# Attention weights in four layers: the clip of the scores replaced by a min with the adjacency

## The reference

```
e   = s1[:, None] + s2[None, :]              # s1 = h @ a1 (rows), s2 = h @ a2 (neighbours), h = relu(layernorm(x)) @ W
e   = where(e > 0, e, 0.2 * e)               # leaky relu
att = softmax(where(adj > 0, e, -9e15), axis=-1)
x   = x + f(att @ h)                         # f: elu (layers 0, 2, 3) or gelu (layer 1); layer 0 then @ W_out + b_out
```

## Time and profile before

| what | us |
|---|---|
| median of three runs | 768.17 (767.72 to 768.95) |
| the profiled execution: its time | 767.65 |
| its span, first to last instruction | 766.0 |
| TensorE busy | 745.2 |
| VectorE busy | 628.0 |
| ScalarE busy | 327.6 |
| mean granted TensorE clock | 0.995 |

### The profile page before, as it was taken

One profiled execution on the slowest core, in us unless ns is written; L12 is line 12 of the kernel. 1 busy time (PEld: TensorE's weight loads), 2 busy tenths in 40 slices (PEclk: granted clock), 3 DMA queues, 4 the chain that ended last, 5 costly groups with the idle time before them and its releaser, 6 DMA issues.

```text
span 766.0 us, 15942 instructions
## 1 busy us (share of the span) xinstructions
PE 745.2 (97%) x6443; PEld 727.3 (95%) x6443; DVE 628.0 (82%) x1050; ACT 327.6 (43%) x886; POOL 16.1 (2%) x36
## 2 busy tenths in 40 slices
PE   8899999999999999999999999999889989998997
PEld 8789999999999999999999999999779979996997
DVE  4997879797787968879787797878688959997986
ACT  5876551452543336134354324633440254435420
POOL 3000000000000000000000000000000000000000
PEclk9999999999999999999999999999999999999999
DMA  9794000000000000000000000000000000000001
GB/s 298 263 357 186 29 28 2 27 0 27 27 1 27 0 27 3 24 27 0 27 12 15 27 0 27 0 0 1 2 1 2 1 1 1 2 1 1 1 22 36
DMA packets 13874, 29.39 MB, mean 38 GB/s; under 512 B 1296, under 2 KB 7568, under 8 KB 13840
## 3 DMA queue, kind: packets, MB, share of 16 engines
q1 hardware_dynamic: 11152, 20.00, 7.6%
q0 software_dynamic: 2688, 8.92, 3.3%
HBM read 27.80 MB, written 1.11 MB: 38 GB/s over the span
## 4 chain that ended last, share of the span: by engine, by line
PE 85%; ACT 5%; DVE 5%; DMA 3%; issue 1%; POOL 0%; DVEq 0%; ACTq 0%; POOLq 0%
PE acc L408 49%; PE acc L431 25%; PE side L508 3%; PE side L364 3%; DMA stage<-in_adj_t_dram 3%; ACT adjT L623 2%; PE acc L378 1%; PE acc L482 1%; DVE probs L1082 1%; ACT hpT L716 1%; PE side L470 1%; DVE stats L1284 0%; PE side L456 0%; DVE xn L1328 0%; ACT fill L701 0%
## 5 line engine op out<-in xcount | busy, mean ns | idle before, releaser
L408 PE MATMUL acc<-V,probs 128*128 128x129 f32 x3840 | 438.3, 276 | 1.9 <-DVE probs L1076 1.9
L408 PEld LDWEIGHTS acc<-V,probs 128*128 128x128 f32 x3840 | 434.2, 192 | 4.9 <-ACT V L657 2.7
L1082 DVE SCALAR_TENSOR_TENSOR probs<-rho,t_now,adjT 128x1024 f32<-128x1024 f32 x224 | 272.9, 1277 | 11.3 <-PE acc L408 9.1
L1178 DVE SCALAR_TENSOR_TENSOR probs<-rho,t_now,adjT 128x768 f32<-128x768 f32 (+3 forms) x179 | 146.7, 879 | 9.6 <-PE acc L431 6.6
L716 ACT ACTIVATE hpT<-rows 32x256 f32<-32x256 f32 x224 | 92.8, 414 | 69.5 <-DVE rows L1119 67.0
L431 PEld LDWEIGHTS acc<-stage,probs 128*128 128x128 f32 x1024 | 115.0, 192 | 4.0 <-ACT stage L874 3.7
L431 PE MATMUL acc<-stage,probs 128*128 128x129 f32 x1024 | 116.1, 275 | 2.1 <-DVE probs L1178 2.1
L431 PE MATMUL acc<-V,probs 128*128 128x129 f32 x768 | 89.4, 275 | 1.0 <-DVE probs L1178 1.0
L431 PEld LDWEIGHTS acc<-V,probs 128*128 128x128 f32 x768 | 87.4, 192 | 2.0 <-ACT V L874 1.8
L701 ACT ACTIVATE fill<-mean_now,empty 128x128 f32<-128x128 f32 x120 | 36.7, 394 | 87.9 <-DVE den L1095 87.8
L1127 DVE TENSOR_TENSOR X<-X,side 128x512 f32<-128x512 f32 x28 | 19.3, 688 | 63.5 <-PE side L508 63.5
(11 more groups left out here) (190 smaller groups left out, 409.4 us busy)
## 6 DMA issues: line engine op xcount, KB each, us to landing
stage<-in_adj_t_dram SPq DMA_DIRECT2D x32, 512.0 KB, 6.7
rho<-rho_dram POOLq DMA_DIRECT2D x15, 512.0 KB, 3.7
X<-in_x_dram SPq DMA_DIRECT2D x2, 512.0 KB, 4.5
W0t<-in_W_t_dram SPq DMA_DIRECT2D x1, 512.0 KB, 5.2
W<-in_L_gnn_W_heads_dram SPq DMA_DIRECT2D x1, 512.0 KB, 6.4
Wout<-in_L_gnn_W_out_dram POOLq DMA_DIRECT2D x1, 512.0 KB, 9.3
out_dram<-X SPq DMA_DIRECT2D x1, 512.0 KB, 4.5
out_dram<-X SPq DMA_DIRECT2D x1, 384.0 KB, 3.9
```

The lines of the kernel that those rows point to most:

```text
L408: last = nc.tensor.matmul(group(c, k), probs[:, j % RING, k * P:(k + 1) * P], V[:, j, :], start=(j == 0 and k % PER_BANK == 0), stop=(j == ...
L1082: nc.vector.scalar_tensor_tensor(probs[:, j % RING, :], rho[:, c * CH:(c + 1) * CH], t_now[:, j:j + 1], adjT[:, j, c * CH:(c + 1) * CH], A ...
L1178: return nc.vector.scalar_tensor_tensor(slot_of(n, p, j)[:, first:end], rho[:, at + first:at + end], t_now[:, j:j + 1], adjT[:, j, at + fi ...
```

## The change

A rho that isn't clipped only exceeds 1 where s1 + c is negative, and there the maximum has to be 1. As adj is 0 or 1 and t is at most 1, the weight can be written as min(max(rho, t), adj). So in all lines that make weights `ALU.mult` becomes `ALU.min`, and:

- rho, t and v come from the scores directly: ScalarE's exponential takes the scores and a bias column -0.8 c or -0.2 c. The VectorE lines 1034 for head 0, 1059, 1065, 1353 and 1364 go (`r_of_first_head`, `r_rows_of_heads`, `exponent_rows`, `late_d`). The maximum is spread with `ident_neg`, -0.8 on the diagonal, and reduced with min to `neg_c`, whose second column is a quarter of it.
- at the start head 0's maximum is spread alone by one matmul, into its own bank. The transposition for the eight heads follows; its second matmul (`spread_max_of_heads`) and `center_of_heads` move behind tiles 1 and 3 of the first unit, and ScalarE's `factors` behind the eighth cast. The cast of block 3 moves behind the first scaling of V.
- v is written straight into V's last column (no copy), and V's first tile is scaled by VectorE.
- the second half of rho comes right behind t and v on ScalarE; the second tile's weights are made in two halves too.
- on TensorE `rows_of_heads(0)` moves from tile 5 to tile 7 and `mean_rows` of the first unit from tile 9 to tile 14.

```diff
+            nc.gpsimd.affine_select(out=ident_neg[:, :], in_=ident_neg[:, :], compare_op=ALU.not_equal, fill=-(1 - ALPHA),
...
             def first_spread_max():
 
                 pe.wait_ge(cmax_ready, 1)
+                pe.wait_ge(ident_neg_ready, 1)
+                pe.wait_ge(first_copied, NB)
+                nc.tensor.matmul(first_max_bank, cmax[:, 0:1].to_broadcast([P, P]), ident_neg[:, :],
+                                 start=True, stop=True).then_inc(first_maxT_psum, 1)
                 nc.tensor.transpose(first_scores[0:H, FT:FT + P], cmax[:, :], ident[:, :]).then_inc(cmaxT_psum, 1)
+
+            def spread_max_of_heads():
+
                 pe.wait_ge(c_row_ready, 1)
...
-            unit(0, 0, 0, ((1, lambda: rows_of_heads(1)), (5, lambda: rows_of_heads(0)),
-                           (9, lambda: mean_rows(1, W0[:, :, :].rearrange("p h d -> p (h d)"), H, r_ready, 6)),
+            unit(0, 0, 0, ((1, spread_max_of_heads), (1, lambda: rows_of_heads(1)), (7, lambda: rows_of_heads(0)),
+                           (14, lambda: mean_rows(1, W0[:, :, :].rearrange("p h d -> p (h d)"), H, rho_ready, 6)),
...
+            def first_factors():
+
+                act.wait_ge(neg_c_ready, 2)
+                nc.scalar.activation(V[:, :, D], s2_all[:, :, 0], ACT.Exp, bias=neg_c_rep[:, 1:2], scale=ALPHA).then_inc(first_vexp, 1)
+                nc.scalar.activation(t_now[:, :], s2_all[:, :, 0], ACT.Exp, bias=neg_c_rep[:, 0:1], scale=1 - ALPHA).then_inc(first_t_ready, 1)
...
             def rho_exp(count, c, heads, which=(0, 1)):
-                r_buf = rho_rows if heads > 1 else rho
+                r_buf, bias = (rho_rows, neg_c_row) if heads > 1 else (rho, neg_c_rep)
+                act.wait_ge(neg_c_ready, 3 if heads > 1 else 1)
                 for k in (2 * c + i for i in which):
-                    act.wait_ge(r_ready, count + k % 2 + 1)
-                    nc.scalar.activation(r_buf[:, k * 512:(k + 1) * 512], r_buf[:, k * 512:(k + 1) * 512], ACT.Exp,
-                                         scale=-(1 - ALPHA)).then_inc(rho_ready, 1)
+                    act.wait_ge(s1_psum, count + k % 2 + 1)
+                    nc.scalar.activation(r_buf[:, k * 512:(k + 1) * 512], side[0:H if heads > 1 else P, k % 2, :], ACT.Exp,
+                                         bias=bias[:, 0:1], scale=-(1 - ALPHA)).then_inc(rho_ready, 1)
...
-            cast(2, 4)
-            factors()
+            cast(2, 3)
             rho_exp(0, 0, 1, (0,))
-            act.wait_ge(tv_ready, 2)
-            nc.scalar.activation(V[:, :, D], v_all[:, 0, :], ACT.Copy)
+            first_factors()
+            rho_exp(0, 0, 1, (1,))
             act.wait_ge(first_copied, NB)
+            act.wait_ge(first_vexp, 1)
             first_scale_v(0)
-            cast(4, 6)
+            cast(3, 6)
             first_scale_v(1)
             cast(6, 8)
+            factors()
...
             def late_factors(n):
 
-                act.wait_ge(late_d_ready, n)
-                nc.scalar.activation(t_now[:, :], late_d[:, :], ACT.Exp, scale=1 - ALPHA).then_inc(late_t_ready, 1)
-                nc.scalar.activation(v_now[:, :], late_d[:, :], ACT.Exp, scale=ALPHA).then_inc(late_vexp_ready, 1)
+                act.wait_ge(late_c_ready, 2 * n - 1)
+                nc.scalar.activation(t_now[:, :], scores[:, :], ACT.Exp, bias=neg_c[:, 0:1], scale=1 - ALPHA).then_inc(late_t_ready, 1)
+                act.wait_ge(late_c_ready, 2 * n)
+                nc.scalar.activation(V_of[n % 2][:, :, D], scores[:, :], ACT.Exp, bias=neg_c[:, 1:2], scale=ALPHA).then_inc(late_vexp_ready, 1)
                 late_rho(n, 0)
+                late_rho(n, 1)
                 act.wait_ge(late_vexp_ready, n)
-                nc.scalar.activation(V_of[n % 2][:, :, D], v_now[:, :], ACT.Copy)
-                scale_late_v(n, 0, 1)
-                late_rho(n, 1)
                 scale_late_v(n, 1, 4)
...
+                dve.wait_ge(first_maxT_psum, 1)
+                nc.vector.tensor_reduce(neg_c_rep[:, 0:1], first_max_bank, AX.X, ALU.min).then_inc(neg_c_ready, 1)
+                dve.wait_ge(neg_c_ready, 1)
+                nc.vector.tensor_scalar(neg_c_rep[:, 1:2], neg_c_rep[:, 0:1], ALPHA / (1 - ALPHA), None, ALU.mult).then_inc(neg_c_ready, 1)
...
+                dve.wait_ge(first_copied, 1)
+                dve.wait_ge(first_vexp, 1)
+                nc.vector.tensor_scalar(V[:, 0, 0:D], V[:, 0, 0:D], V[:, 0, D:D + 1], None, ALU.mult).then_inc(first_v, 1)
...
-            unit(0, 0, rho_and_adj(0, 0, True), ((5, lambda: r_rows_of_heads(1)), (6, lambda: mean(0, 1)), (9, lambda: r_rows_of_heads(0)), (12, add_bias),
-                                                   (15, first_t)), t_all[:, 0, :])
+            unit(0, 0, rho_and_adj(0, 0, True), ((3, center_of_heads), (6, lambda: mean(0, 1)), (12, add_bias)))
...
             def late_center(n):
 
                 dve.wait_ge(late_maxT_psum, n)
-                link(nc.vector.tensor_reduce(late_c[:, :], max_bank, AX.X, ALU.max))
-                nc.vector.tensor_scalar(late_d[:, :], scores[:, :], late_c[:, 0:1], None, ALU.subtract).then_inc(late_d_ready, 1)
-
-            def exponent_rows(n, k):
...
+                nc.vector.tensor_reduce(neg_c[:, 0:1], max_bank, AX.X, ALU.min).then_inc(late_c_ready, 1)
+                dve.wait_ge(late_c_ready, 2 * n - 1)
+                nc.vector.tensor_scalar(neg_c[:, 1:2], neg_c[:, 0:1], ALPHA / (1 - ALPHA), None, ALU.mult).then_inc(late_c_ready, 1)
+                dve.wait_ge(late_vexp_ready, n)
+                v0 = V_of[n % 2][:, 0, :]
+                nc.vector.tensor_scalar(v0[:, 0:D], v0[:, 0:D], v0[:, D:D + 1], None, ALU.mult).then_inc(late_v0_ready, 1)
```

More of the change, by code:

```diff
@@ L396, in unit @@
                         pe.wait_ge(rows_ready, 2 * u - 1)
-                    first = j == 0 and isinstance(u, int) and u == 0
-                    if first:
+                    first = j < 2 and isinstance(u, int) and u == 0
+                    if first and j == 0:
                         pe.wait_ge(first_v, 1)
-                        pe.wait_ge(first_half, 1)
                     elif c == 0 and (j % 4 == 0 or isinstance(u, int) and u == 0 and j == 1):
                         pe.wait_ge(v_ready, q * 4 + j // 4 + 1)
-                    if not first:
+                    if first:
+                        pe.wait_ge(first_half, j + 1)
+                    else:
                         pe.wait_ge(probs_ready, u * NT + j + 1)
@@ L653, in first_scale_v @@
             def first_scale_v(g):
-                for t in range(4 * g, 4 * g + 4):
+                for t in range(max(4 * g, 1), 4 * g + 4):
                     where = V[:, t, 0:D] if t < NK + 1 else first_group(t)[:, 0:D]
[L657 to L660, removed]
+                    last = nc.scalar.activation(V[:, t, 0:D], where, ACT.Copy, scale=V[:, t, D:D + 1])
                 last.then_inc(v_ready, 1)
+            def first_factors():
+                act.wait_ge(neg_c_ready, 2)
+                nc.scalar.activation(V[:, :, D], s2_all[:, :, 0], ACT.Exp, bias=neg_c_rep[:, 1:2], scale=ALPHA).then_inc(first_vexp, 1)
+                nc.scalar.activation(t_now[:, :], s2_all[:, :, 0], ACT.Exp, bias=neg_c_rep[:, 0:1], scale=1 - ALPHA).then_inc(first_t_ready, 1)
             def factors():
@@ L865, in late_rho @@
                 to = rho[:, k * 512:(k + 1) * 512]
-                act.wait_ge(late_r_ready, 4 * (n - 1) + k + 1)
-                nc.scalar.activation(to, to, ACT.Exp, scale=-(1 - ALPHA)).then_inc(late_rho_ready, 1)
+                if k < 2:
+                    act.wait_ge(s1_kept, 2 * n - 1 + k)
+                    s1_rows = to
+                else:
+                    act.wait_ge(late_s1_psum, 4 * (n - 1) + k + 1)
+                    s1_rows = side[:, k % 2, :]
+                nc.scalar.activation(to, s1_rows, ACT.Exp, bias=neg_c[:, 0:1], scale=-(1 - ALPHA)).then_inc(late_rho_ready, 1)
             def scale_late_v(n, first, end):
@@ L1073, in unit @@
                         dve.wait_ge(summed, u * NT + j - RING + 1)
-                    if j == 0 and isinstance(u, int) and u == 0:
-                        dve.wait_ge(rho_ready, 1)
-                        nc.vector.scalar_tensor_tensor(probs[:, 0, 0:512], rho[:, 0:512], t_now[:, 0:1], adjT[:, 0, 0:512],
-                                                       ALU.max, ALU.mult).then_inc(first_half, 1)
-                        dve.wait_ge(rho_ready, 2)
-                        nc.vector.scalar_tensor_tensor(probs[:, 0, 512:CH], rho[:, 512:CH], t_now[:, 0:1], adjT[:, 0, 512:CH],
-                                                       ALU.max, ALU.mult).then_inc(probs_ready, 1)
+                    if j < 2 and isinstance(u, int) and u == 0:
+                        if j == 0:
+                            dve.wait_ge(first_t_ready, 1)
+                        for k, done in enumerate((first_half, probs_ready)):
+                            dve.wait_ge(rho_ready, k + 1)
```

(8 more changed lines are left out.)

91 lines of the change are left out of this document (42 added, 49 removed).

## The result

The changed kernel takes 769.44 us (median of 20 runs, 767.57 to 772.61), the kernel before 767.63 in the 20 runs beside them: ratio 1.0025, interval 1.0017 to 1.0033. I had forecast 766.8 and held anything above 768.4 unlikely. Beside the later experiments both were timed again: 1.0019 (1.0009 to 1.0030). One execution of the start's part with the mean's row after tile 9 (experiment 3) fell into a slow state, 1288 us at a granted clock of 0.557, and its ratio leaves it out.

What follows compares the result with a forecast made beforehand. TensorE, busy 745 of 766 us, bounds the kernel; only its roughly 20 us of standing can give. Late layers 0.9 plus hpT 0.5 make 1.4 us off 768.17, so 766.8; range 765.3 to 768.4.

Steps and rivals of the forecast that it cites:

- The late layers: Three late layers' beginnings: first tile 0.16 us earlier, second tile's 0.14 us stall gone; 0.30 a layer, 0.9 in all.
- The bias's price: ScalarE's exponentials: a bias column adds 0.08 to 0.09 us each; the 512-wide one takes 709 ns against 626.
- The start up to the first tile: First unit: rho on ScalarE at 20.36 instead of 21.77, TensorE's first weighted matmul near 22.45, 1.0 us earlier.
- rival A: Clock stays up at the start, bias costs nothing: late layers 1.4 us, ScalarE's chain 1.0 to 1.6 earlier; 765.4; chance 0.22.
- The wait for the mean's row: ScalarE in the first unit waits 2.7 to 4.4 us for the row moved behind later tiles, holding back casts and loads.
- its effect on hpT: Before the first output projection: hpT comes 0.3 to 0.7 us earlier, 0.5 taken, and TensorE carries that lead.
- my case without a fall: Start with the clock not fallen: mean's row done at 55.1, ScalarE ready by 52.4, waiting 2.7 us.
- The load of block 27: Start's load for the 28th block: issued at 59.2, must land within 3.8 us; estimated 3.3 us, in time.
- The step that failed: Start: TensorE's 1.0 us lead at the first tile can't be kept, as it already stands for hpT at 81.88.
- Rival C: Start: waiting for the mean starves the loads, the 28th block lands 3.7 us later; 2.8 us slower, 771.0; chance 0.10.

Runs made afterwards that it cites:

- experiment 3: Changed lines put into the kernel before by part: start's 770.31 us, late layers' 766.55 us, start's with the mean's row after tile 9 766.39 us.
- late only: Only the late layers' part of the change put into the kernel before: 766.55 us, 0.9987.
- version 6: Changed kernel with the mean's row after tile 9 and useless matmuls in two standstills of each late layer: 764.06 us, 0.9944; again 763.97 us, 0.9952.
- experiment 2: Kernel before with only the first unit's mean's row moved from after tile 9 to after tile 14: 772.23 us, 1.0047.
- the start alone: Only the start's part of the change put into the kernel before: 770.31 us, 1.0034.
- experiment 1: Changed kernel with the first unit's mean's row after tile 9 instead of tile 14: 765.05 us, 0.9963 of the kernel before.

## Why the prediction was wrong

Where the time of the profiled executions goes, cut at four kinds of instruction (us; a star: the clock fell in it):

| stretch | before | change | mean's row at 9 | late only | before, row at 14 | version 6 |
|---|---|---|---|---|---|---|
| to the first projection | 81.88* | 81.61 | 78.61 | 81.55* | 86.17* | 80.23* |
| to the first late spread | 476.86* | 478.26* | 476.81* | 476.71 | 478.26* | 477.51* |
| spread to second tile, layer 1 | 5.26 | 5.25* | 4.94 | 5.52* | 5.56* | 4.94 |
| the same, layer 2 | 5.25 | 5.52* | 6.42* | 4.94 | 5.56* | 4.94 |
| the same, layer 3 | 5.25 | 4.94 | 4.94 | 4.94 | 5.25 | 4.94 |
| first late spread to the end | 207.2 | 207.0 | 208.0 | 206.6 | 207.9 | 206.1 |
| span | 766.0 | 766.8 | 763.5 | 764.9 | 772.3 | 763.8 |

The falls in the first row lie near 24 us (before, row at 14) or 12 us (late only, version 6). Those in the second lie near 550 us, ahead of the late layers, and cost little, but for the two of 478.26, which have theirs behind the first projection.

**The late layers: right where the clock stays up, which in the change it does in one layer of three.** Predicted 0.30 us a layer, as 0.16 at the first tile and 0.14 at the second. Where the clock stays up it is 5.25 to 4.94 = 0.31, as 0.17 and 0.14. The terms are in the rows of the third late layer: reduce at 702.44, t_now at 702.76 (0.31 us, 0.21 without a bias), rho at 703.18, half tile at 704.03, TensorE at 704.92, which is 3.08 us after the spread instead of 3.25. The bias's price is that of the rows:

```profile
L901 ACT ACTIVATE rho<-rho,neg_c 128x512 f32<-128x512 f32 x6 | 4.0, 708 | 0.0
```

708 ns against 626, an Exp now, so the Trainium skill's rule ("ScalarE: Activation LUTs", section "What ACT_TABLE_LOAD costs"), some 93 ns for each pointer operand, holds for it within 11 ns. As a whole the late part gave 1.0 us in experiment 3, against 0.9 predicted. What I left out of it is the clock: in the beginnings of layers 1 and 2 it fell in all three profiles of the change, and there the exponent scores (four matmuls, 1.9 us) take 3.0 to 3.5 and end last instead of the half tile. So from the first late spread to the end the three profiles of the change gain 0.2 to 0.3 us on the one of before, not 0.9.

```profile
630.51 0.49 PE L520 MATMUL acc<-ident_neg,late_max 128*128 128x128 f32 x2 [0.40 <-DVE late_max L1376]
630.83 3.52 PE L512 MATMUL side<-hT,waL 128*128 128x512 f32 x4
634.14 2.28 PE L453 MATMUL acc<-V,probs 128*128 128x129 f32 x18
```

In the kernel before, its one profile has no fall there, but the profiles of experiment 2 and of the start alone, both with the late layers of before, have two each, so I can't say that the change makes them more frequent.

**The start up to the first tile: right.** Predicted: rho at 20.36, half tile near 21.55, TensorE near 22.45, ninth cast at 31.4. Measured 20.36, 21.57, 22.47, 31.31:

```profile
20.36 0.69 ACT L700 ACTIVATE rho<-side,neg_c_rep 128x512 f32<-128x512 f32 x1 [0.83 <-DVE neg_c_rep L1064]
...
21.57 2.74 DVE L1115 SCALAR_TENSOR_TENSOR probs<-rho,t_now,adjT 128x512 f32<-128x512 f32 x4
...
22.47 3.81 PE L428 MATMUL acc<-V,probs 128*128 128x129 f32 x32 [1.50 <-DVE probs L1115]
```

The clock didn't fall behind the shorter standstill, so TensorE won another 1.3 us. My forecast had worked out both cases; rival A (0.22) counted on this one.

**The wait for the mean's row: right in place, and its effect on hpT near.** Predicted 2.7 to 4.4 us of wait, measured 4.66: the row was done as in my case without a fall (55.59, I had 55.1), but ScalarE stood ready at 50.9 and not 52.4, so the wait is 2 us longer than the 2.7 I had for that case. Block 22's cast came at 57.05 (58.3 predicted), block 27's at 61.97 (63.0), hpT 0.3 us earlier (0.3 to 0.7; in the other two profiles of the change 0.4 earlier and not at all). The load of block 27 took 3.8 us, an estimated 3.3 in the prediction; the fixed cost in that estimate is one that the Trainium skill ("DMA: Bandwidth & Descriptors", section "Anatomy of one DMA") gives for DMAs issued by GpSimd, while SyncE issues these. Then the last two casts wait for their loads, 0.8 us in all, where I had them back to back:

```profile
67.74 1.06 ACT L647 ACTIVATE adjT<-stage 128x1024 bf16<-128x1024 int32 x1 [0.48 <-DMA stage<-in_adj_t_dram]
69.15 1.06 ACT L647 ACTIVATE adjT<-stage 128x1024 bf16<-128x1024 int32 x1 [0.35 <-DMA stage<-in_adj_t_dram]
```

**The step that failed** is the sentence "TensorE near 22.45: 1.0 us earlier. But TensorE then has a lead it can't keep: at 81.88 it stands already for hpT". It priced the lost lead at nothing. A lead that can't be kept is a longer standstill, 1 us to 3, and behind it the clock falls in a stretch that has no slack: 1.4 us in the profile. With it the account of the profile closes: 1.4 us faster were predicted, 0.8 slower came; of these 2.2 us the fall takes 1.4, the late layers' missing gain 0.6 and hpT's 0.2. And the lead could be kept: with the row after tile 9 (experiment 1) nothing of it is lost, so the standstill was the price of the moved row. I had the fall at 24 us in front of me and asked only whether it would come again at the start, where it costs nothing; I didn't ask where the next standstill goes. Rival C named the right place, the wait for the mean starving the loads, but let it pay through a late block 27, and I gave it a chance of 0.10. In the change that load came in time and the next ones cost 0.8 us. Experiment 2 shows how near the edge the forecast stood: there ScalarE comes to the wait at 53.9 and not 50.9, the row comes 2.4 us later too (TensorE starts its tiles 1.1 us later and its clock falls at 24 us), and rival C's mechanism makes 2.9 us of waits for loads.

**What stays open.** By profile the change is 0.8 us slower, by median 1.8 (20 runs) and 1.4 (12 runs). So some 0.6 to 1 us of the loss is in no profile, and the account above doesn't cover it. The granted clock of the 20 runs goes from 0.988 to 0.995, that of the profiled ones is 0.993, and the runs with the lower clock are the longer ones (correlation -0.68), so falls of the clock play a part; falls in the late layers at other places, as the 6.42 us of the table, are of the right size. But the mean clock of the kernel before is the same 0.992 to 0.993 in its runs: the change doesn't have more falls, so they would have to lie where they cost more. That was not settled run by run.

## What to carry to other kernels

When an edit brings one engine earlier to a meeting point that another one holds, nothing is won there and the standstill grows: follow the engine that comes last there through every job queued on it, and ask what the longer standstill does to TensorE's clock in the stretch behind it. An aside whose result another engine waits for is on the path of that engine: here one such line, moved five tiles down, cost 4 us and turned a gain of 0.4% into a loss. A standstill that can't be removed may be worth filling with useless matmuls.

## What the runs showed of the hardware

- TensorE's clock went to 1.2 GHz for 3.4 us after standstills of 2.1 us (before, at 23.45), 3.0 to 3.3 (change, three times, and its start alone) and 4.0 (experiment 2). After 0.4 to 1.4 us at the same projection it stayed up, and after 2.1 us too (four useless matmuls). So 2.1 us were followed by a fall once and once not.
- It also fell in the late layers' beginnings, where no wait is over 1.8 us but short waits and short groups of matmuls alternate. The fall comes late: in the change TensorE stands from 78.6 to 81.6 and the clock falls at 81.4.
- The same 512 KB loads came at other distances in each execution: the last cast started at 68.8 to 70.1 us for the same program but for what stands behind it. The first weighted matmul started at 22.4 to 22.8 us, and at 23.1 in the two executions whose clock had fallen at 12.2 us.
- A bias column cost a 512-wide exponential 82 ns (708 against 626) and a 16-wide one 0.1 us (0.31 against 0.21).
